# Cross-attention with group norm on one core: group statistics in one product per batch, taken around a pivot

## The reference

```
q = Wq y + bq ; k = Wk y + bk ; v = Wv x + bv          # 8 heads of 16 channels
attn = softmax( q k^T / sqrt(128) )                    # 16 x 16 per head, over channels
o = Wo (attn v) + bo + x
mu, var = mean(o), var(o)                              # over all 128 x 1024 values of the batch
out = (o - mu) * rsqrt(var + 1e-5) * gn_w + gn_b
```

## Time and profile before

| | |
|---|---|
| median of 3 runs | 175.67 us (175.47 to 176.19) |
| the profiled execution | 175.87 us, of which the span from first to last instruction is 174.1 us |
| TensorE busy | 163.0 us (94%), 997 matmul records |
| VectorE busy | 151.8 us (87%), 555 instructions |
| ScalarE busy | 135.8 us (78%) |
| GpSimd busy | 112.4 us (65%) |
| DMA | 50.70 MB, mean 291 GB/s; 81.0% of the queues' share |
| granted TensorE clock | 0.988 of full speed in the mean (9 tenths or more in 39 of 40 slices, the last at 5) |

### The profile page before, as it was taken

One profiled execution on the slowest core, in us unless ns is written; L12 is line 12 of the kernel. 1 busy time (PEld: TensorE's weight loads), 2 busy tenths in 40 slices (PEclk: granted clock), 3 DMA queues, 4 the chain that ended last, 5 costly groups with the idle time before them and its releaser, 6 DMA issues. The chain is left out here.

```text
span 174.1 us, 4168 instructions
## 1 busy us (share of the span) xinstructions
PE 163.0 (94%) x997; PEld 129.2 (74%) x997; DVE 151.8 (87%) x555; ACT 135.8 (78%) x356; POOL 112.4 (65%) x166
## 2 busy tenths in 40 slices
PE   7989999999999999999999999999999999999730
PEld 7877888877777888877777778888777777785410
DVE  1786999999998999999999999999999999976551
ACT  4656588998878888798888888888988888776442
POOL 3287677877866777776787677767778777741020
PEclk9999999999999999999999999999999999999995
DMA  6998778999899999989999999999999866622223
GB/s 206 409 416 339 254 224 322 328 334 334 279 355 336 311 330 321 332 308 342 334 314 325 356 324 326 313 333 330 330 339 327 297 237 241 242 121 120 121 115 126
DMA packets 14265, 50.70 MB, mean 291 GB/s; under 512 B 1712, under 2 KB 1712, under 8 KB 14256
## 3 DMA queue, kind: packets, MB, share of 16 engines
q1 hardware_dynamic: 13968, 50.34, 81.0%
q10 hardware_dynamic: 288, 0.27, 0.5%
HBM read 33.82 MB, written 16.78 MB: 291 GB/s over the span
## 5 line engine op out<-in xcount | busy, mean ns | idle before, releaser
L514 PE MATMUL o_ps<-x_sb,m_sb 128*128 128x512 f32 x128 | 63.1, 615 | 0.0
L431 DVE TENSOR_TENSOR hl_sb<-y_sb,hl_sb 128x512 fp32r<-128x512 f32 x64 | 47.9, 749 | 1.7 <-ACT hl_sb L326 1.0
L271 POOL TENSOR_TENSOR rstd<-veps,nhalf 128x1 f32<-128x1 f32 x32 | 28.2, 882 | 24.5 <-DVE veps L436 24.5
L326 ACT CAST hl_sb<-y_sb 128x512 fp32r<-128x512 f32 x64 | 39.5, 620 | 1.8 <-DMA y_sb<-in_ctx_dram 1.8
L514 PE MATMUL g_ps<-hl_sb 128*128 128x258 f32 x256 | 38.6, 293 | 0.0
L366 ACT ACTIVATE out_sb<-o_ps,shift,gain 128x1024 f32<-128x1024 f32 (+1 forms) x32 | 38.3, 1197 | 0.1
L300 POOL TENSOR_TENSOR lsuma<-hl_sb 128x256 f32<-128x256 f32 x31 | 23.2, 749 | 22.9 <-DVE hl_sb L431 22.9
L514 PEld LDWEIGHTS o_ps<-x_sb,m_sb 128*128 128x128 f32 x128 | 22.1, 191 | 14.9 <-issue 14.0
L514 PEld LDWEIGHTS g_ps<-hl_sb 128*128 128x128 f32 x256 | 32.8, 190 | 0.0
L321 ACT ACTIVATE a_sb<-sc_sb,smin 128x128 f32<-128x128 f32 x32 | 12.9, 402 | 16.8 <-DVE smin L422 16.7
L287 POOL TENSOR_TENSOR lsum<-lsuma,lsumb 128x256 f32<-128x256 f32 x31 | 22.8, 737 | 4.1
(11 more groups left out here) (64 smaller groups left out, 297.6 us busy)
## 6 DMA issues: line engine op xcount, KB each, us to landing
y_sb<-in_ctx_dram SPq DMA_DIRECT2D x32, 512.0 KB, 5.1
x_sb<-in_x_dram SPq DMA_DIRECT2D x32, 512.0 KB, 5.6
out_dram<-out_sb SPq DMA_DIRECT2D x31, 512.0 KB, 4.8
out_dram<-out_sb SPq DMA_DIRECT2D x2, 256.0 KB, 2.2
w_in<-in_weights_dram ACTq DMA_DIRECT2D x1, 256.0 KB, 5.4
cols<-in_columns_dram ACTq DMA_DIRECT2D x1, 3.0 KB, 3.3
```

Source lines behind the costliest of these rows:

```text
L271: nc.gpsimd.tensor_tensor(rstd[:, h1:h1 + 1], veps[:, h1:h1 + 1], nhalf[:, :], ALU.pow).then_inc(rstd_ready, 1)
L326: nc.scalar.copy(hl_sb[:, k, chunks, 0:C], y_sb[:, k, chunks, :]).then_inc(h_ready, 1)
L431: nc.vector.tensor_tensor(hl_sb[:, ky, chunks, C:2 * C], y_sb[:, ky, chunks, :], hl_sb[:, ky, chunks, 0:C].bitcast(F32), ALU.subtract).the ...
L514: return nc.tensor.matmul(dst, lhsT, rhs, start=start, stop=stop, **more)
```

## The change

The mean and variance of a batch are no longer taken one after the other. A pivot is taken first, from M, c and the first column of `x`: on each partition the accumulated sum of that partition's row of the stored matrix (`colsum`) times `x[:, 0]`, plus c (`st_in[..., 2]`), summed over the partitions; that is minus the mean of one column of `o`. The statistics of the batch are then taken around it: `st_in[..., 0]` is the channel mean plus c minus the pivot, `st_in[..., 1]` its square plus the channel variance. One product (`statistics`) sums these two columns of batch `t-4` together with the pivot column of batch `t-3`, three columns in one product per step. The variance is then the summed squares less the square of the summed deviation (`nvar`, `veps`).

On the engines:

- TensorE: `mean` and `variance` go, `statistics` comes, behind the scores. `softmax_product` goes ahead of `query_product`, and the folded matrix's two products go between the two halves of the Gram products.
- VectorE: `mrow`, `dev` and `vrow` go. `st_in[0]`, `st_in[1]`, the pivot, `nvar` and `cp` come. The copy of M becomes an operation with an accumulated row sum (128 columns), and column E is copied by one of its own. The copy of the scores, `zinv` and `g_sb` move from the head of the next step to the tail of this one; the copy of M moves from the tail to just behind `bn_aggr`.
- ScalarE: `round_half(0)` moves from behind the exponential to behind the copy of `r_sb`.
- SyncE and GpSimd: no line changes.

```diff
--- before.py
+++ after.py
         mv = sb("mv", [P, 2, 2])
-        mrow = sb("mrow", [P, 2])
-        dev = sb("dev", [P, 2])
-        vrow = sb("vrow", [P, 2])
+        colsum = sb("colsum", [P, 2])
+        st_in = sb("st_in", [P, 2, 3])
+        cp = sb("cp", [P, 2])
+        nvar = sb("nvar", [P, 2])
...
-        mu_ps, var_ps, s_ps = st_ps[:, 0:1], st_ps[:, 8:9], g_ps[:, 2 * C:2 * C + 1]
+        s_ps = g_ps[:, 2 * C:2 * C + 1]
...
-        mrow_ready = sem("mrow_ready")
-        mu_ready = sem("mu_ready")
+        pivot_ready = sem("pivot_ready")
-        vrow_ready = sem("vrow_ready")
-        var_ready = sem("var_ready")
+        q_ready = sem("q_ready")
+        st_ready = sem("st_ready")
+        nvar_ready = sem("nvar_ready")
...
                 def round_half(half):
                     chunks = slice(half * HCH, (half + 1) * HCH)
                     nc.scalar.copy(hl_sb[:, k, chunks, 0:C], y_sb[:, k, chunks, :]).then_inc(h_ready, 1)
-                if has(t, 0):
-                    act.wait_ge(y_in[k], slot_count(t0, k, 0))
-                    if exists(t, 4):
-                        act.wait_ge(g_ready, t - 3)
-                    round_half(0)
                 if has(t, 3):
                     act.wait_ge(zinv_ready, t - 2)
@@ -356,6 +351,13 @@
                     act.wait_ge(r_ready, t - 2)
                     nc.scalar.copy(r_sb[:, :], r_ps).then_inc(r_copied, 1)
+                if has(t, 0):
+                    act.wait_ge(y_in[k], slot_count(t0, k, 0))
+                    if exists(t, 4):
+                        act.wait_ge(g_ready, t - 3)
+                    round_half(0)
...
-                def folded_matrix():
-                    dve.wait_ge(m_ready, t - 2)
-                    nc.vector.tensor_tensor(m_sb[:, h1, :], m_ps, ident[:, :], ALU.add).then_inc(m_copied, 1)
-                if has(t, 3):
-                    done = value(t - 2)
-                    dve.wait_ge(const_dve, 10)
-                    dve.wait_ge(sc_ready, done)
-                    nc.vector.tensor_tensor_reduce(out=sc_sb[:, :], in0=sc_ps, in1=k0[:, :], scale=1.0,
-                                                   scalar=3e38, op0=ALU.add, op1=ALU.min,
-                                                   accum_out=smin[:, h1:h1 + 1]).then_inc(smin_ready, 1)
                 def rest_half(b, half):
                     ky = (k + b) % UNROLL
@@ -431,43 +418,32 @@
                     nc.vector.tensor_tensor(hl_sb[:, ky, chunks, C:2 * C], y_sb[:, ky, chunks, :],
                                             hl_sb[:, ky, chunks, 0:C].bitcast(F32), ALU.subtract).then_inc(l_ready, 1)
-                def variance():
-                    dve.wait_ge(var_ready, t - 4)
-                    nc.vector.tensor_scalar(veps[:, h1:h1 + 1], var_ps, -1.0, EPS, ALU.mult, ALU.add).then_inc(veps_ready, 1)
-                if has(t, 5):
-                    variance()
+                if has(t, 2):
+                    dve.wait_ge(g_ready, t - 1)
+                    nc.vector.tensor_copy(s_sb[:, :], s_ps).then_inc(s_copied, 1)
                 if has(t, 1):
                     rest_half(-1, 1)
-                if has(t, 2):
-                    dve.wait_ge(g_ready, t - 1)
-                    nc.vector.tensor_tensor(g_sb[:, :], g_ps[:, 0:C], b2_sb[:, :].bitcast(F32), ALU.add).then_inc(g_copied, 1)
-                    nc.vector.tensor_copy(s_sb[:, :], s_ps).then_inc(s_copied, 1)
-                if is_step(t, 2):
-                    dve.wait_ge(rows_copied, 2)
-                    nc.vector.scalar_tensor_tensor(out=k0[:, :], in0=bkB[:, :], scalar=bq_col[:, :],
-                                                   in1=mask[:, :, :].rearrange("p h d -> p (h d)"),
-                                                   op0=ALU.mult, op1=ALU.add).then_inc(const_dve, 1)
-                if has(t, 3):
-                    dve.wait_ge(exp_done, t - 2)
                 if has(t, 4):
                     dve.wait_ge(o_ready, (t - 4) * 2 + 1)
                     nc.vector.bn_stats(bn[:, h, 0, :], o_ps[:, h, 0:HALF])
                     dve.wait_ge(o_ready, (t - 3) * 2)
                     nc.vector.bn_stats(bn[:, h, 1, :], o_ps[:, h, HALF:L]).then_inc(bn_done, 1)
-                if is_step(t, RUSH):
-                    folded_matrix()
...
                     dve.wait_ge(s_copied, t - 1)
                     dve.wait_ge(p_ready, t - 1)
                     nc.vector.scalar_tensor_tensor(out=p_sb[:, :], in0=bqB[:, :], scalar=s_sb[:, :],
                                                    in1=p_ps, op0=ALU.mult, op1=ALU.add).then_inc(p_copied, 1)
+                if is_step(t, 2):
+                    nc.vector.scalar_tensor_tensor(out=k0[:, :], in0=bkB[:, :], scalar=bq_col[:, :],
+                                                   in1=mask[:, :, :].rearrange("p h d -> p (h d)"),
+                                                   op0=ALU.mult, op1=ALU.add).then_inc(const_dve, 1)
@@ -475,24 +451,70 @@
                     dve.wait_ge(bn_done, done)
                     nc.vector.bn_aggr(mv[:, h, :], bn[:, h, :, :].rearrange("p a b -> p (a b)")).then_inc(mv_ready, 1)
                     dve.wait_ge(mv_ready, t - 3)
-                    nc.vector.tensor_scalar(mrow[:, h:h + 1], mv[:, h, 0:1], m_sb[:, h, E:E + 1], None,
-                                            ALU.add).then_inc(mrow_ready, 1)
+                    nc.vector.tensor_tensor(st_in[:, h, 0:1], mv[:, h, 0:1], cp[:, h:h + 1], ALU.add).then_inc(dev_ready, 1)
+                if has(t, 3):
+                    done = value(t - 2)
+                    dve.wait_ge(const_dve, 10)
+                    dve.wait_ge(m_ready, done)
+                    nc.vector.tensor_tensor_reduce(out=m_sb[:, h1, 0:E], in0=m_ps[:, 0:E], in1=ident[:, 0:P], scale=1.0,
+                                                   scalar=0.0, op0=ALU.add, op1=ALU.add, accum_out=colsum[:, h1:h1 + 1])
+                    nc.vector.tensor_tensor(m_sb[:, h1, E:E + 1], m_ps[:, E:E + 1], bo, ALU.add).then_inc(m_copied, 1)
+                if has(t, 4):
+                    dve.wait_ge(dev_ready, t - 3)
+                    nc.vector.tensor_scalar(st_in[:, h, 1:2], st_in[:, h, 0:1], st_in[:, h, 0:1], mv[:, h, 1:2],
+                                            ALU.mult, ALU.add).then_inc(q_ready, 1)
+                if has(t, 3):
+                    kx = (k - 3) % UNROLL
+                    dve.wait_ge(x_in[kx], slot_count(t0, k, 3))
+                    dve.wait_ge(m_copied, t - 2)
+                    nc.vector.scalar_tensor_tensor(out=st_in[:, h, 2:3], in0=colsum[:, h1:h1 + 1],
+                                                   scalar=x_sb[:, kx, 0:1], in1=m_sb[:, h1, E:E + 1],
+                                                   op0=ALU.mult, op1=ALU.add).then_inc(pivot_ready, 1)
                 if has(t, 0):
                     rest_half(0, 0)
+                if has(t, 2):
+                    done = value(t - 1)
+                    dve.wait_ge(const_dve, 10)
+                    dve.wait_ge(sc_ready, done)
+                    nc.vector.tensor_tensor_reduce(out=sc_sb[:, :], in0=sc_ps, in1=k0[:, :], scale=1.0,
+                                                   scalar=3e38, op0=ALU.add, op1=ALU.min,
+                                                   accum_out=smin[:, h:h + 1]).then_inc(smin_ready, 1)
+                if has(t, 3) or has(t, 4):
+                    dve.wait_ge(st_ready, t - 2)
                 if has(t, 4):
-                    dve.wait_ge(mu_ready, t - 3)
-                    nc.vector.tensor_tensor(dev[:, h:h + 1], mrow[:, h:h + 1], mu_ps, ALU.add).then_inc(dev_ready, 1)
+                    nc.vector.tensor_scalar(nvar[:, h:h + 1], st_ps[:, 0:1], st_ps[:, 0:1], st_ps[:, 1:2],
+                                            ALU.mult, ALU.add).then_inc(nvar_ready, 1)
+                if has(t, 3):
+                    nc.vector.tensor_tensor(cp[:, h1:h1 + 1], m_sb[:, h1, E:E + 1], st_ps[:, 2:3], ALU.add)
+                if has(t, 4):
                     if exists(t, 6):
                         dve.wait_ge(affine_ready, t - 5)
-                    nc.vector.scalar_tensor_tensor(out=wshift[:, h:h + 1], in0=mu_ps, scalar=m_sb[:, h, E:E + 1],
+                    nc.vector.scalar_tensor_tensor(out=wshift[:, h:h + 1], in0=st_ps[:, 0:1], scalar=cp[:, h:h + 1],
                                                    in1=gn_w, op0=ALU.add, op1=ALU.mult)
-                    dve.wait_ge(dev_ready, t - 3)
-                    nc.vector.tensor_scalar(vrow[:, h:h + 1], dev[:, h:h + 1], dev[:, h:h + 1], mv[:, h, 1:2],
-                                            ALU.mult, ALU.add).then_inc(vrow_ready, 1)
-                if has(t, 3) and not is_step(t, RUSH):
-                    folded_matrix()
+                    dve.wait_ge(nvar_ready, t - 3)
+                    nc.vector.tensor_scalar(veps[:, h:h + 1], nvar[:, h:h + 1], -1.0, EPS,
```

(53 more changed lines are left out.)

6 lines of the change are left out of this document (3 added, 3 removed).

## The result

| | before | after |
|---|---|---|
| median | 175.67 us (175.25 to 176.61, 17 runs) | 175.07 us (174.46 to 177.44, 17 runs) |
| ratio | 1 | 0.995, 95% interval 0.9933 to 0.9967 |
| profiled execution | 175.87 us, span 174.1 | 175.22 us, span 173.4 |

A forecast was written before the change was run, and what follows sets the result against it. TensorE was taken as full at 4.73 us a step; after the change VectorE's floor of 4.64 bounds, step 4.66. Gains 2.2 + 0.4 + 0.6 = 3.2 us take 175.87 to 172.7, median 172.5; range 168.5 to 179.0.

The forecast's parts named there:

- The steady step: Middle of the loop: a step goes from 4.73 to 4.66 us, 2.2 us over 31 distances.
- a ring through ScalarE: Middle of the loop: moving `round_half(0)` closes a ring from `r_sb` through `x` and softmax, 4.61 us, hidden below VectorE's floor.
- the order, not the work, bounds: Sign of being wrong: `nvar` waits for its product, or VectorE and TensorE both wait; time above 175 us.
- The loop's bubble stays: End of each loop turn: the excess over the steady step was taken to remain unchanged.
- The start-up has idle engines and gets neither: First steps: engines are idle there, so neither the saving nor the cost was counted.
- The last batch: From its second `bn_stats` to `veps`: the path falls from 1.62 to 1.26 us, a gain of 0.4.
- The three distances before it: Three steps before the last batch: one product less on the path, 3 x 0.24, of which 0.6 us taken.
- VectorE dearer: Rival, steady step: VectorE pays 4.76 to 4.84 us a step, time 175.6 to 178.1 us; chance 0.25.
- TensorE alone: Rival, steady step: TensorE alone decides at 4.49 us, 8.4 us go, time 167.3 us; chance 0.07.
- No saving on TensorE: Rival: split Gram row and later waits eat the 0.24; step stays 4.73, time 174.7 us; chance 0.05.
- Collision of `rstd`: Rival: GpSimd's power `rstd` and VectorE's second subtraction hold each other up; 4.93 a step, 180.9 us; chance 0.15.

The follow-up runs named there:

- f1: e9 with the folded matrix's products behind three of the eight Gram products instead of four; 171.30 us, ratio 0.9762 against the kernel before.
- e5: Kernel after with VectorE's loop boundary alone moved behind the first subtraction of a step; 174.24 us, ratio 0.9949 against the kernel before.
- e7: Kernel after with TensorE's loop boundary alone moved behind the products of `x`; 174.61 us, ratio 0.9933 against the kernel before.
- e6: Kernel after with both VectorE's and TensorE's loop boundaries moved; 173.40 us, ratio 0.9852 against the kernel before.
- e3: Kernel before with VectorE's steps all written out instead of looped; 175.04 us, ratio 0.9944 against the kernel before.
- e8: Kernel before with TensorE's loop boundary alone moved behind the products of `x`; 176.57 us, ratio 1.0051 against the kernel before.
- e4: Kernel after with batch 1's second subtraction back in step 1, ahead of `g_sb`; 173.73 us, ratio 0.9918 against the kernel before.
- e9: Kernel after with the edits of e4 and e6 together; 172.01 us, ratio 0.9786 against the kernel before.

## Why the prediction was right or wrong

**The steady step: right.** Forecast 4.66, measured 4.65 to 4.66. Its terms: `st_in[0]`, column E and `cp` were given 0.07 each, and take 0.12 (in f1), 0.07 and 0.06; the square 0.19 (0.18 forecast), `nvar` 0.20 (0.18), the pivot 0.13 to 0.14 (0.13), copy of M 0.22 with a free read (0.22). VectorE's floor is 4.61 (f1), forecast 4.64, and there is luck in this. What came sums to 0.77 and not 0.70, which would have made 4.71; operations that the change leaves as they are took 0.10 less than in the kernel before (`veps` 0.06 for 0.10, the two `bn_stats` 0.60 each for 0.61 and 0.62, the rest in hundredths). TensorE's floor is 4.54, forecast 4.49: the eight Gram products take 0.57 + 0.57 in halves, where the undivided row took 1.04 to 1.05, so the split costs 0.10 and not 0 to 0.05.

**The bound's name: wrong, at little cost.** I wrote down a ring through ScalarE (4.61) and not the one that the change itself makes: copy of M, pivot, `statistics`, `x`, softmax, folded matrix, 4.65. I had treated the wait for the pivot as a wait of TensorE beside a full VectorE, "about 0.15 a step"; it is 0.12, but VectorE waits too, 0.03 to 0.04 behind `st_in[0]` (0.15 to 0.16 against 0.12 in f1). A part of the miss is a hand-over: from the end of the pivot to `statistics` it is 0.14 (102.10 to 102.24), where I had 0.05. Both engines waiting is the sign that I had given for "the order, not the work, bounds", with a time above 175; the time came, but not by the steady step. The wrong name changed nothing in the sum only because 4.61, 4.64 and 4.65 are so close.

**"The loop's bubble stays": wrong.** This is the first step that failed. I took the excess at the turn's end as a constant of the loop, and it is none: 0.28 became 0.52, and its size depends on what stands at the boundaries of VectorE and TensorE. Over the loop's turns that is 0.9 us of 2.2: the 31 distances would have given 2.2 and the three last ones 0.3, and gave 1.60. e5, e7 and e6 show it for the kernel after: with both boundaries moved the turn is 18.69, against 18.64 for four steps of 4.66. Why the same edge cost only 0.28 before isn't shown. That slack hid the rest is my reading; e3 and e8, which gave back 0.11 and nothing there, don't settle it.

**"The start-up has idle engines and gets neither": wrong, and the larger error.** An idle engine can't start what stands behind a wait in its queue. The move of `g_sb` to the tail of step 1, ahead of the second subtraction of batch 1, cost 1.3 us in the profiles (17.88 to 19.16); putting the subtraction back returned 1.2 in e4 and 0.9 in e9, counted from the start of batch 1. I had listed the moves for the loop only and not followed them through the first two steps.

**The last batch: right.** -0.4 forecast; second `bn_stats` to `veps` is 165.69 to 168.01, 2.32 against 2.67. The three distances before it gave 13.65 to 13.18, 0.47, of which 0.21 is the general 0.07: 0.26 where I had taken 0.6 from a span of 0 to 0.8.

Added up: -2.2, -0.3 and -0.4, and +0.9 and +1.3 that I had at nothing, make -0.7, as the two spans show. With these two repaired, e9 has 172.0, where the forecast was 172.5. That is no proof of the forecast, since e9 also removes the bubble that the kernel before has: before with both its boundaries hidden was not run, and I can't say how much of e9's 3.7 us belongs to the statistics. The terms that touch neither boundary add up to 2.9: 2.2 of the steady steps (4.73 against 4.66) and 0.7 at the end.

**The rivals.** *VectorE dearer*: refuted, 4.61. *TensorE alone*: refuted, the step didn't fall to 4.49. *No saving on TensorE*: its time of 174.7 is the nearest to the result, but of its mechanism only the 0.10 of the split row is there, and the step didn't stay at 4.73; a time that fits doesn't vouch for a cause. *Collision of `rstd`*: here it stands 0.08 ahead of the subtraction, and neither pays (timelines of GpSimd and VectorE of after):

```profile
98.87 0.55 POOL L271 TENSOR_TENSOR rstd<-veps,nhalf 128x1 f32<-128x1 f32 x1
...
98.95 0.68 DVE L418 TENSOR_TENSOR hl_sb<-y_sb,hl_sb 128x512 fp32r<-128x512 f32 x1
```

Over the whole run `rstd` fell from a mean of 0.882 to one of 0.547. The lead was forecast at 0.11. The Trainium skill (SBUF — State Buffer, section "SBUF: two separate sides") lets the one that starts first hold the ports for its whole length; for this one-column power these rows do not show that, here as in the earlier trace rows.

## What to carry to other kernels

When a change takes the slack out of an engine, don't carry the loop's bubble over as a constant: look at the place of each engine's loop boundary and put it behind the longest queued operation, on all the engines that share the edge, since one alone gained little here (0 and 0.15 us a turn, both together 0.45). Follow every moved operation through the start-up too: behind which wait does it stand in the first two steps? And after a sum by engines, write down each ring that the new waits close, with its hand-overs; here it was within 0.04 us of the engine's work.
